# Head attention of a fused transformer block: two output transposes spread over two key tiles, with the projections' slots, GpSimd's order and the look-ahead of the row scores moved to suit

## The reference

```python
# per sequence (8 of them): target = layernorm(x), source = ctx, both 256 x 512
q = einsum('oc,bct->bot', Wq, target) + bq      # 16 heads of 16 channels, 512 positions
k = einsum('oc,bcs->bos', Wk, source) + bk
v = einsum('oc,bcs->bos', Wv, source) + bv
dot = einsum('bhdt,bhds->bhts', q, k) / sqrt(16)
dot = mask * dot - (1 - mask) * 1e6
amap = softmax(dot, axis=-1) * mask
x = x + einsum('bhts,bhds->bhdt', amap, v)      # all but the last sum is "head attention"
```

## Time and profile before

| | us |
|---|---|
| median of 3 runs | 1424.12 (1423.53 to 1425.8) |
| profiled execution, its own time | 1422.36 |
| its span, first to last instruction | 1420.5 |
| mean granted TensorE clock | 0.972 of full |
| TensorE busy | 1299.8 (92%) |
| VectorE busy | 1002.7 (71%) |
| ScalarE busy | 648.5 (46%) |
| GpSimd busy | 300.1 (21%) |

### The profile page before, as it was taken

The page is one execution under the profiler, slowest core; times in us unless marked ns, Lnnn a source line. Parts: engine busy times, 40 slices in busy tenths (PEclk is TensorE's granted clock), DMA queues, the critical chain, the costliest instruction groups (busy, mean ns, idle before and its releaser), DMA issues.

```text
span 1420.5 us, 23319 instructions
## 1 busy us (share of the span) xinstructions
PE 1299.8 (92%) x9113; PEld 755.5 (53%) x9142; DVE 1002.7 (71%) x1523; ACT 648.5 (46%) x941; POOL 300.1 (21%) x473
## 2 busy tenths in 40 slices
PE   5787969899899999978999899999999999999998
PEld 2343412232232332225767667777767867777776
DVE  8989778888888898875768846635466444675353
ACT  5675627888888888862632111232112311112210
POOL 1008346466465564210000000000000000000000
PEclk9999969999999999988999999999999999999999
DMA  6300222433334332245544101000010000101000
GB/s 203 110 19 16 71 80 66 119 98 112 107 101 145 102 112 85 61 149 179 189 117 143 62 30 60 30 2 1 30 62 10 22 1 30 60 1 30 1 1 30
DMA packets 78038, 101.23 MB, mean 71 GB/s; under 512 B 14679, under 2 KB 51647, under 8 KB 77927
## 3 DMA queue, kind: packets, MB, share of 16 engines
q1 hardware_dynamic: 75879, 99.43, 22.1%
q0 software_dynamic: 2048, 0.27, 0.1%
HBM read 78.07 MB, written 21.34 MB: 70 GB/s over the span
## 4 chain that ended last, share of the span: by engine, by line
PE 42%; DVE 8%; DMA 1%; issue 1%; ACT 1%; POOL 1%; POOLq 0%; DVEq 0%; SPq 0%; ACTq 0%
PE double L1803 13%; PE double L1817 11%; PE double L1829 6%; PE double L1882 3%; PE double L1850 3%; PE double L1839 3%; PE double L1869 1%; PE double L1787 1%; DVE stats L1990 1%; DMA x_early<-scr_x 1%; DVE hid L2037 1%; DVE gate L2035 1%; DMA out_x<-x_early 1%; DVE x_early L2006 1%; POOL rstd L1976 1%
## 5 line engine op out<-in xcount | busy, mean ns | idle before, releaser
L1030 ACT ACTIVATE prob<-level,head_scale 128x512 f32<-128x512 f32 x512 | 317.9, 681 | 77.9 <-PE level L947 76.4
L1392 DVE TENSOR_REDUCE nmx<-level 128x2 f32<-128x1024 f32 x256 | 306.6, 1221 | 49.6 <-PE level L937 49.2
L1915 ACT ACTIVATE th<-double 128x512 f32<-128x512 f32 x96 | 53.9, 561 | 385.9 <-PE double L1803 212.7
L947 PE MATMUL level<-stacks 59*128 59x512 f16 x512 | 173.8, 390 | 10.7 <-ACT prob L1030 10.7
L1976 POOL TENSOR_TENSOR rstd<-meanvar,halfpow 128x2 f32<-128x2 f32 x22 | 15.2, 691 | 689.4 <-DVE meanvar L1996 689.4
L937 PE MATMUL level<-stacks 57*128 57x512 f16 x512 | 152.2, 394 | 8.4 <-DVE nmx L1392 8.3
L374 PE MATMUL level<-prob,x_parts 128*128 128x448 bf16 (+1 forms) x527 | 124.2, 388 | 37.2 <-DVE prob L421 16.9
L1803 PE MATMUL double<-x_parts,f0w 128*128 128x256 f16 x1408 | 156.6, 274 | 1.6 <-PEq L521 1.6
L1803 PE MATMUL double<-x_parts,f1w 128*128 128x256 f16 x1408 | 155.2, 273 | 0.4 <-DVE hid L2037 0.4
L1803 PEld LDWEIGHTS double<-x_parts,f0w 128*128 128x128 bf16 x1408 | 138.4, 98 | 20.6 <-issue 2.5
L1803 PEld LDWEIGHTS double<-x_parts,f1w 128*128 128x128 bf16 x1408 | 137.5, 98 | 18.5 <-DVE hid L2037 0.7
(11 more groups left out here) (254 smaller groups left out, 1866.0 us busy)
## 6 DMA issues: line engine op xcount, KB each, us to landing
stacks<-scr_q SPq DMA_DIRECT2D x64, 96.0 KB
stacks<-scr_k SPq DMA_DIRECT2D x64, 96.0 KB
hid<-in_f1w1t SPq DMA_DIRECT2D x8, 704.0 KB, 6.0
hid<-in_f1w2t SPq DMA_DIRECT2D x8, 704.0 KB, 4.3
inputs<-in_x SPq DMA_DIRECT2D x8, 512.0 KB, 7.2
inputs<-in_ctx SPq DMA_DIRECT2D x8, 512.0 KB, 6.9
scr_q<-splits SPq DMA_DIRECT2D x16, 256.0 KB, 2.4
scr_k<-splits SPq DMA_DIRECT2D x16, 256.0 KB, 2.3
```

The source lines that it names most:

```text
L947: nc.tensor.matmul(pB[n % 2], Ks[rows, g, j // 2, P * c:P * (c + 1)], Qs[rows, g, j // 2, :], start=True, stop=True).then_inc(s["b_pe"], 1)
L1030: nc.scalar.activation(prob[:, c, j, :], pB[(64 * b + 16 * g + 4 * c + j) % 2], ACT.Exp, scale=hscale[:, 10:11]).then_inc(s["exp_done"], 1)
L1392: nc.vector.tensor_reduce(nmx[:, g % 2, :, half, tt], pA[(32 * b + 8 * g + u // 2) % 2], AX.X, ALU.max, negate=True).then_inc(s["max_done" ...
L1915: y = nc.scalar.activation(th[:, 0:m, :], src[:, 0:m, 0:S], ACT.Tanh, scale=0.5 / XS)
```

## The change

In words: the second transpose job "o" leaves the second half of unit (1, 0) and gets unit (1, 2). The jobs behind it move by one unit or more: "t" of group 0 to (1, 3), "q" part 1 to (2, 0), "k" part 1 to (2, 3), "v" to (3, 0) and (3, 3), so that each of the 16 units has one job, in its first half. ScalarE's and VectorE's readers move with them. `row_units` is now counted by halves: the row scores stand 14 units in front instead of 12, so that a group's last pair is made in the first half of unit (g, 0), and `max_parts` comes there too. On VectorE the two residual sums are at (1, 0) and (1, 2). On GpSimd the split of k part 1 goes from group 2 to group 3, that of q part 1 from group 1 to group 2, and `c_parts` from group 2 to group 1. SP's program is unchanged. (The numbering of the lines below 688 shifts by 9 to 11.)

```diff
--- before.py
+++ after.py
@@ -635,13 +635,12 @@
 
         MISC = {
             (0, 0): [("q", 0, 1), None], (0, 1): [("nm", 1, 0), None], (0, 2): [("t", 3, -1), None], (0, 3): [("k", 0, 1), None],
-            (1, 0): [("o", 0, -1), ("o", 1, -1)], (1, 1): [("nm", 2, 0), None], (1, 2): [("t", 0, 0), None],
-            (1, 3): [("q", 1, 1), None],
-            (2, 0): [("k", 1, 1), None], (2, 1): [("nm", 3, 0), None], (2, 2): [("t", 1, 0), None], (2, 3): [("v", 0, 1), None],
-            (3, 0): [("v", 1, 1), None], (3, 1): [("nm", 0, 1), None], (3, 2): [("t", 2, 0), None],
+            (1, 0): [("o", 0, -1), None], (1, 1): [("nm", 2, 0), None], (1, 2): [("o", 1, -1), None], (1, 3): [("t", 0, 0), None],
+            (2, 0): [("q", 1, 1), None], (2, 1): [("nm", 3, 0), None], (2, 2): [("t", 1, 0), None], (2, 3): [("k", 1, 1), None],
+            (3, 0): [("v", 0, 1), None], (3, 1): [("nm", 0, 1), None], (3, 2): [("t", 2, 0), None], (3, 3): [("v", 1, 1), None],
         }
 
-        PROJECTED = {(0, 0): (0, 0), (0, 3): (0, 1), (1, 3): (1, 0), (2, 0): (1, 1)}
+        PROJECTED = {(0, 0): (0, 0), (0, 3): (0, 1), (2, 0): (1, 0), (2, 3): (1, 1)}
 
         LAST = {(2, 1): [None, ("rep", 0, 0)], (2, 3): [None, ("one", 0, 0)], (3, 0): [("x", 0, 0), None],
                 (3, 1): [("top", 0, 0), None], (3, 3): [("spread", 0, 0), None]}
@@ -679,25 +678,17 @@
         def present(job, first, last):
             return job is not None and not (job[2] < 0 and first) and not (job[2] > 0 and last)
 
-        def row_units(b, g, c):
-
-            ahead = g + 1 if c == 0 else g + 2
+        def row_units(b, g, c, half):
+
+            ahead = g + 1 if c == 0 and half == 0 else g + 2
             nb, ng = (b, ahead) if ahead < NG else (b + 1, ahead - NG)
-            return nb, ng, 12 if c == 0 else 4 * (c - 1), ahead >= NG
+            return nb, ng, (4 * c + 2 * half - 2) % 16, ahead >= NG
 
         def row_unit(u):
 
 
             j = u % 4 ^ 1
             return j % 2, j // 2, u // 4
...
 
         block = ctx.enter_context(nc.Block())
 
@@ -966,7 +957,7 @@
                 row_scores(0, 0, u)
             run("nm", 0, 0)
             run("v", 1, 0)
-            for u in range(12):
+            for u in range(14):
                 row_scores(0, 1, u)
 
             pe.wait_ge(W["turned_act"], W["turns"])
@@ -975,13 +966,13 @@
                 for g in range(NG):
                     for c in range(DK):
 
-                        nb, ng, u0, next_one = row_units(b, g, c)
                         jobs = MISC.get((g, c), [None, None])
                         for half in range(2):
+                            nb, ng, u0, next_one = row_units(b, g, c, half)
                             column_scores(b, g, c, 2 * half)
                             if not (last and next_one):
-                                row_scores(nb, ng, u0 + 2 * half)
-                                row_scores(nb, ng, u0 + 2 * half + 1)
+                                row_scores(nb, ng, u0)
+                                row_scores(nb, ng, u0 + 1)
                             column_scores(b, g, c, 2 * half + 1)
                             if half == 1:
                                 if c:
@@ -1201,10 +1192,8 @@
             def body(b, first, last, ending):
 
                 for g in range(NG):
-                    if not last and g == 0:
-                        split(b + 1, 0, (0,))
-                    if not last and g == 2:
-                        split(b + 1, 1, (1,))
+                    if not last and g != 1:
+                        split(b + 1, int(g >= 2), (int(g == 3),))
                     if g < NG - 1:
                         max_rows(b, g + 1)
                     elif not last:
@@ -1213,13 +1202,13 @@
                         value_group(b, g + 1)
                     elif not last:
                         value_group(b + 1, 0)
+                    if not last and g == 0:
+                        split(b + 1, 0, (1,))
                     if g == 1 and not ending:
                         ln_pow(b + 2)
-                    if not last and g < 2:
-                        split(b + 1, g, (1 - g,))
+                        c_parts(b + 2)
                     if g == 2 and not ending:
                         x_parts(b + 2)
-                        c_parts(b + 2)
                     if g >= 2 and last:
                         ln_pow(B + g - 2)
 
@@ -1461,24 +1450,24 @@
             max_parts(0, 0)
             v_evac(0, 1)
             ln_apply(1)
-            maxima(0, 1, 0, 12)
+            maxima(0, 1, 0, 14)
 
             def body(b, first, last, ending):
                 for g in range(NG):
                     for c in range(DK):
-                        nb, ng, u0, next_one = row_units(b, g, c)
                         for half in range(2):
+                            nb, ng, u0, next_one = row_units(b, g, c, half)
                             if not (last and next_one):
-                                maxima(nb, ng, u0 + 2 * half, 2)
-                                if u0 + 2 * half == 14:
+                                maxima(nb, ng, u0, 2)
+                                if u0 == 14:
                                     max_parts(nb, ng)
-                            if c == 2 and half == 0:
+                            if c == (3 if g == 1 else 2) and half == 0:
                                 if g:
                                     normalise(b, g - 1)
                                 elif not first:
                                     normalise(b - 1, NG - 1)
-                            if g == 1 and c == 0 and not first:
-                                residual(b - 1, (half,))
+                            if g == 1 and c in (0, 2) and half == 0 and not first:
+                                residual(b - 1, (c // 2,))
                             if last and half:
                                 if (g, c) == (2, 0):
                                     scale_peaks()
@@ -1501,8 +1490,8 @@
                                     dense_norm(1)
                                 elif (g, c) == (3, 3):
                                     attention_scales()
-                            if (g, c) in ((2, 3), (3, 0)) and half == 0 and not last:
-                                v_evac(b + 1, g - 2)
+                            if (g, c) in ((3, 0), (3, 3)) and half == 0 and not last:
+                                v_evac(b + 1, c // 3)
                         if g == 0 and c == 3 and not ending:
                             ln_stats(b + 2)
                         if g == 1 and c == 3 and not ending:
```

6 lines of the change are left out of this document (removed).

## The result

| | before | after |
|---|---|---|
| median, us | 1423.37 (8 runs) | 1431.65 (8 runs, 1428.33 to 1434.81) |
| ratio | | 1.0065 (95% interval 1.0053 to 1.0077) |
| profiled execution; its span, us | 1422.36; 1420.5 | 1430.68; 1428.8 |
| mean granted clock | 0.972 | 0.968 |

A forecast was written before the change was run, and what follows sets the result against it. VectorE was taken to bound the stretch from (1, 0) to (1, 1). Terms -2.6, -1.9, -1.5, -1.1 (sequences) and +1.1 (start) sum to -6.0, taken as -5.8 from 1424.1: 1418.3 us, range 1415.5 to 1423.2.

The forecast's parts named there:

- VectorE is the bound: From the values of (1, 0) to those of (1, 1): 5.51 us, in which VectorE works 5.44 and TensorE 3.12.
- its chain of 4.56 us: VectorE's serial maximum, parts, residual, maximum behind the statistics; values of (1, 1) start at 333.35 instead of 334.29, 0.94 us less.
- With less idle time before it, I expect the clock to hold: In (1, 1) of sequences 0 and 4, the 3.4 us stretches at clock 0.50 vanish, gaining 0.9 us each.
- The tight place on the queue: "k" part 1 moves to (2, 3) and fill 2 depends on it; it fits by 1.2 us or is 0.2 late.
- Rival A: Fill 2 late, TensorE waiting in the second half of (0, 0); 1428.1 us at a lag of 1.5; chance 0.12.
- The sum of 14.4 to 15.8 us against 15.6: From the start of (3, 0): time until fill 2 lands, against when the next sequence's row scores need it.
- half of cases: In (2, 0), VectorE's parts come behind GpSimd's split of "q" and wait; TensorE loses 0.2 us a sequence.
- Rival C: In head attention, TensorE's idle time only moves, VectorE's chain is longer, clock drops still come: 1422.5 us; chance 0.13.
- The start: Before the loop, VectorE bound: two more row units in front are one more pair, so +1.1 us.
- Sequences 6 and 7: Without statistics, the 3.86 us stretch becomes 3.06 + 0.2, 0.6 us less; 1.1 us gained for both.
- The second "o" in (1, 2): The moved job needs 0.6 us on TensorE in a unit waiting for ScalarE's exps; claimed to cost nothing.
- Rival B: VectorE, blocked behind GpSimd in (2, 0), becomes the bound: 0.6 instead of 0.2 us in seven sequences, 1421.1 us; chance 0.15.

The follow-up runs named there:

- e3_k22: Changed kernel with "k" part 1 in (2, 2), "t" behind it in (2, 3), and GpSimd's split of k ahead of `x_parts`: 1415.78 us, ratio 0.9953.
- e4_loads: Changed kernel with the loads of context and x of a later sequence moved behind fill 1: 1423.84 us, ratio 1.0005.
- e5_both: Changed kernel with the edits of e3_k22 and e4_loads together: 1415.28 us, ratio 0.994.
- e6_both_warm: e5_both plus repeated row scores, result unused, where TensorE waits for VectorE: 1415.6 us, ratio 0.9941.
- e18_before_add_late: Kernel before with only the small operation on 128 x 2 variances moved behind (1, 1), the aggregation staying: 1418.19 us, ratio 0.9966.
- e1_warm: Changed kernel with TensorE repeating row scores, result unused, where it waits for VectorE in (1, 1): 1426.82 us, ratio 1.0019.
- e8_both_warm12: e6_both_warm with row scores 12 units in front and the repeats at the matching pairs: 1415.2 us, ratio 0.995.
- e13_late_var: e5_both with the statistics' aggregation and the variances' operation moved behind (1, 1): 1408.42 us, ratio 0.9891.
- e14_late_var12: e13_late_var with row scores 12 units in front: 1406.98 us, ratio 0.9884.
- e16_spread_late: e13_late_var with the first statistics instruction moved behind (0, 1): 1411.82 us, ratio 0.9918.
- e7_before14: Kernel before with only the look-ahead of 14 units and `max_parts` in the first half of (g, 0): 1431.45 us, ratio 1.0044.
- e2_look12: Changed kernel with row scores 12 units in front again: 1424.78 us, ratio 1.0019.
- e15_before_late_var: Kernel before with only the aggregation and the variances' operation moved behind (1, 1): 1413.22 us, ratio 0.9931.

## Why the prediction was wrong

**"VectorE is the bound", and its chain of 4.56 us: right in length, wrong in cause.** Where x was in time and the clock held, (1, 1) took 4.58 us in 12 of 15 sequences and 4.94 in three (e3_k22, e4_loads, e5_both, e6_both_warm). With 3.06 us in (1, 0) that is the 0.94 us less that I forecast for the two units. But the chain hangs on the start of the maximum, which I took as given: "the layer-norm statistics hold it from 326.91 to 329.41, 2.50 us". Of these, 1.20 us are the statistics, some 0.4 the aggregation, and 0.9 a tiny operation standing until GpSimd's split is done. I had the row and its cause in hand, and priced it only at (2, 0), where the change added an operation. It is worth more where it already stood: 1.05 us a sequence (e18_before_add_late). In the changed kernel, where VectorE runs later, it is an operation on 128 x 1 elements just ahead of it that is held, for 0.52 to 1.06 us in sequences 1, 2, 3 and 5.

The Trainium skill (SBUF — State Buffer, "SBUF: two separate sides") restricts the shared port pair to certain VectorE operations: those in a two-port mode, or with two inputs in SBUF while GpSimd's operation reads SBUF. The traces agree, but for one case left open (beside GpSimd's 128 x 64 operations the same TENSOR_SCALAR took 0.17 us). The tiny operations, one with two inputs in SBUF, one a TENSOR_SCALAR, were held until GpSimd's operation ended (0.52, 0.57, 0.99, 1.05 and 1.14 us instead of 0.17 or less), while beside the same split the statistics took 0.64 us each (1.28 for two) and the maximum, read from PSUM, 1.21, as elsewhere.

**"With less idle time before it, I expect the clock to hold": this step failed, and cost most.** It was an expectation with no row behind it. The sum of idle time in (1, 0) and (1, 1) did fall, from 2.4 us in each of sequences 1 to 3 to 1.8, 1.4 and 1.7, and the granted clock went to 0.50 in all three, where it had held, and for twice as long in 4. e1_warm, which fills the idle time with useless matmuls, prices it at 6.9 us in (1, 0) to (1, 2), about half of the 13 us between forecast and result. What decides that the clock falls is open: with the same idle stretches it fell in sequence 1 of the changed kernel and held in 5, and fell in 5 of e5_both and held in 1, 2 and 4. Shown is that it held in all of sequences 1 to 6 of the kernels that leave TensorE at most one idle stretch over 0.25 us in these units, of 1.22 us or less (e6_both_warm, e8_both_warm12, e13_late_var, e14_late_var12, e16_spread_late). The shares of clock, x and fill 2 overlap and can't be added: e3_k22, which moves k alone, gains 15.9 us.

**The tight place on the queue: seen in part.** Rival A came true: fill 2 late in (0, 0), +4.3 us over eight sequences. The sum of 14.4 to 15.8 us against 15.6 said as much, and I charged 0.1 us a sequence, the friendly end. In sequence 2 the scores of (3, 0) begin at 359.44 and fill 2 at 364.83, 5.4 us later, as summed; but its stacks release TensorE only at 375.83, 11.0 us behind, where I had 9 to 10.4. What I missed comes behind fill 2. I followed the mask row and not x. Fill 3 and x keep their place in SP's order, and fill 3 its time, but they now meet fill 2 and its followers on the way: one issue takes up to 1.4 us longer, and x up to 2.3 us longer to land. That the meeting is the cause is an inference, which e3_k22 supports. The statistics waited 4.7 us for x in five waits, and (1, 1) of sequence 4 became 8.3 us. e4_loads heals the wait for x, e3_k22 that for fill 2 and most of the other. The two effects fed the clock: with the lags mended (e5_both) only one half-clock stretch is left between 213 and 626 us.

**Rival C** ("the idle time only moved, the clock drops still come") named the mechanism and gave it 1422.5 us, since it counted the two drops that were there and no new ones. The chance for slower was 0.09.

**The start** was right in these two executions: +1.1 us forecast, +1.2 measured. From the first row scores to the first column score it is 22.2 to 23.3 us in the kernels with 14 units in front and 21.2 to 22.2 with 12, and 0.6 to 2.2 us within a pair. But the look-ahead costs more than the start: e7_before14 is 0.44% slower than before, and e2_look12 6.9 us faster than the change.

**Sequences 6 and 7** gained 0.6 us each in (1, 0) and (1, 1), as forecast, and lost 0.4 to 0.6 of it in (0, 0). **The second "o" in (1, 2)** cost nothing: in e5_both (1, 2) is 3.06 us. **Rival B** came true as an event: I took half of cases, and in (2, 0) of each of sequences 0 to 5 one operation of the parts was held, for 1.13 to 1.24 us, and in (3, 0) of 0 to 6 for 0.86. But TensorE saw only 0.2 us of it ((2, 1) at 3.46 instead of 3.27 us), the 0.2 us a sequence that I had put in; it became visible once the rest was gone (e13_late_var). VectorE and GpSimd in sequence 2:

```profile
348.98 1.13 DVE L1391 SCALAR_TENSOR_TENSOR nmp<-nmx,nmp 128x16 f16<-128x16 f32 x1
```

```profile
348.81 1.27 POOL L1093 TENSOR_TENSOR splits<-splits,mrow 128x512 f32<-128x512 f32 x1 [4.65 <-ACT splits L1004]
```

The transposes' move seems sound: e13_late_var and e14_late_var12 are 4.8 and 6.2 us below e15_before_late_var in the medians. Some of that is not the move's, since these two also load x earlier, and sequence 4's wait for x, 1.4 us, is in e15_before_late_var alone; the other jobs stand elsewhere too. The move by itself was never run. The loss came with its company: k's late slot with the loads that it crowds, and the look-ahead of 14.

Open: what the 1.91 us issue on SP waited for (with fill 2 earlier, in e3_k22, it takes 0.47), and what lets the clock fall in one sequence and hold in the next.

## What to carry to other kernels

Before pricing a busy engine's chain, look for tiny operations with long durations in it, and for the operation of another engine that ends at the same instant: such time is a wait, and a tiny operation may be easy to move. When a transfer's condition moves later, list all that its queue does behind it and all that will be on the way together with it, and who waits for each, to the end of the period. And where TensorE's idle time is moved and not removed, price the clock for each period as if it may fall there: at the lower level the values took 1.93 us instead of 1.07.

## What the runs showed of the hardware

A VectorE operation on 2 to 16 elements a partition (TENSOR_SCALAR, or SCALAR_TENSOR_TENSOR with two inputs in SBUF) took 0.17 us beside a free GpSimd and up to 1.24 us (0.99 to 1.14 in the rows shown) when it began beside GpSimd's 128 x 512 operation, whose end it kept to within 0.03 us; beside GpSimd's 128 x 64 operations (four in 1.19 us, e13_late_var) it took 0.17 us. BATCH_NORM_AGGREGATE, 0.17 us, was never held. Idle stretches of TensorE of at most 0.52 us each stood before a fall of the granted clock to 0.50 (e5_both, sequence 5), while 1.43 and 0.96 us stood in sequences 1 to 3 of the kernel before at 1.00. Useless matmuls in such gaps made a kernel 4.8 us faster. A 512 KB load of x took 7.1 to 8.1 us to land in the kernel before and 8.9 to 9.4 us in the changed one (sequences 1, 2, 3 and 5), where earlier transfers are still on the way when fill 3 begins.
